# First stage of a filter-and-spectrum kernel on one core: tails and row transform in one PSUM pair ahead of the second column block, normalisation mid-step, input loaded and measured four images at a time

## The reference, cut to what matters

```
x = x + L0(gn(x), f)          # layer 0: the first stage of the kernel
x = x + L1(gn(x), a1 .. d2)   # layer 1: spectrum of gn(x), small complex products, inverse spectrum

gn(v):   mean and variance over groups of 4 channels (32 groups), (v - m) / sqrt(s + 1e-5)
L0(v,f): upsample by 2 with a 12-tap filter, columns then rows -> 266 x 266
         y = y if y >= 0 else 0.01 * y
         filter and keep every second sample, columns then rows -> 128 x 128
```

## Time and profile before

| | us |
|---|---|
| time, median of 3 runs | 5614.12 (5610.11 to 5619.64) |
| the profiled execution's own time | 5615.34 |
| its span, first to last instruction | 5613.4 |
| PE / DVE / ACT / POOL busy in the span | 4717.3 / 3792.0 / 3255.8 / 2574.6 |
| first stage: first and last step's `Z` instruction (L615, 256 of them) start at | 46.2 and 3137.5 |
| TensorE's clock granted over the span | 0.966 of full speed |

### The profile page before, as it was taken

How to read it: one execution, slowest core, us unless ns; L and a number is a source line. 1 busy time by engine, 2 the same in 40 slices (tenths; PEclk the granted TensorE clock), 3 DMA queues, 4 the chain that set the end, 5 groups by cost and what they waited for, 6 DMA issues and landing times. The chain is left out here.

```text
span 5613.4 us, 246109 instructions
## 1 busy us (share of the span) xinstructions
PE 4717.3 (84%) x103206; PEld 4285.6 (76%) x103206; DVE 3792.0 (68%) x5737; ACT 3255.8 (58%) x5654; POOL 2574.6 (46%) x2950
## 2 busy tenths in 40 slices
PE   6788787887787787888888769999999999998999
PEld 5777777777777777777777658888888888888999
DVE  5666666666666666666666588888888888884333
ACT  5655655656556656556565356666666666663332
POOL 5665656656656656656566133333333333331000
PEclk9999999999999999999999789999999999999999
DMA  1113132131131131131311412222222222225999
GB/s 52 48 48 96 48 89 62 48 96 48 57 97 48 48 104 48 55 89 48 103 49 46 140 46 75 75 75 75 75 71 69 69 75 75 75 75 227 420 421 399
DMA packets 606871, 555.75 MB, mean 99 GB/s; under 512 B 14916, under 2 KB 540228, under 8 KB 589508
## 3 DMA queue, kind: packets, MB, share of 16 engines
q1 hardware_dynamic: 606276, 546.68, 29.5%
HBM read 278.19 MB, written 268.44 MB: 97 GB/s over the span
## 5 line engine op out<-in xcount | busy, mean ns | idle before, releaser
L1278 DVE TENSOR_TENSOR Ml<-ring,Mh 128x1024 f16<-128x1024 f32 x1024 | 1199.5, 1219 | 200.5 <-ACT Mh L1245 192.9
L1245 ACT ACTIVATE Mh<-ring 128x1024 f16<-128x1024 f32 x1024 | 987.0, 1023 | 301.1 <-PE ring L1179 300.5
L753 DVE SCALAR_TENSOR_TENSOR Y<-ring,Y 128x532 f16<-128x532 f32 x1024 | 680.4, 706 | 680.1 <-ACT Y L604 680.1
L604 ACT ACTIVATE Y<-ring 128x532 f16<-128x532 f32 x1024 | 573.1, 612 | 897.6 <-PE ring L361 897.6
L345 PE MATMUL ring<-uth,g 64*128 64x138 f16 x6144 | 458.1, 227 | 545.7 <-DVE Zt L776 379.6
L1179 PE MATMUL ring<-wcur,b_hi 64*128 64x128 f16 x16384 | 747.9, 217 | 177.8 <-DVE Ml L1278 138.5
L262 POOL TENSOR_TENSOR A<-Af,A 128x788 f16<-128x788 f32 x512 | 861.9, 1683 | 41.3
L345 PEld LDWEIGHTS ring<-uth,g 64*128 64x128 f16 x6144 | 331.3, 97 | 624.8 <-DVE Yt L772 419.0
L1179 PEld LDWEIGHTS ring<-wcur,b_hi 64*128 64x128 f16 x16384 | 609.7, 94 | 248.1 <-DVE Ml L1278 156.2
L1179 PE MATMUL ring<-wcur,b_lo 64*128 64x128 f16 x8192 | 715.5, 216 | 0.0
L361 PE MATMUL ring<-uth,A 64*128 64x138 f16 x12288 | 581.7, 225 | 29.0 <-issue 25.5
(11 more groups left out here) (153 smaller groups left out, 10927.3 us busy)
## 6 DMA issues: line engine op xcount, KB each, us to landing
xb<-in_x SPq DMA_DIRECT2D x128, 512.0 KB, 4.1
x<-x1b SPq DMA_DIRECT2D x64, 1024.0 KB, 7.0
spec<-sp_out SPq DMA_DIRECT2D x256, 256.0 KB, 3.4
xin<-spec SPq DMA_DIRECT2D x128, 512.0 KB, 6.6
fd<-ft SPq DMA_DIRECT2D x128, 512.0 KB, 4.4
F<-fd SPq DMA_DIRECT2D x64, 1024.0 KB, 20.1
xq<-x SPq DMA_DIRECT2D x64, 1024.0 KB, 16.9
out<-yq SPq DMA_DIRECT2D x64, 1024.0 KB, 18.5
```

What stands on the lines that cost most here:

```text
L604: act.activation(Y[:, e, 0, m], ring[:, pr[u], :, 0:UPS], ACT.Relu).then_inc(e_yh, 1)
L753: dve.scalar_tensor_tensor(out=Y[:, e, 1, m], in0=ring[:, pr[u], :, 0:UPS], scalar=0.0, in1=Y[:, e, 0, m], op0=ALU.max, op1=ALU.subtract). ...
L1245: act.activation(hi, ps, ACT.Copy).then_inc(e_hi, 1)
L1278: dve.tensor_tensor(lo, ps, hi, ALU.subtract).then_inc(e_lo, 1)
```

## The change

Five things are changed in `phase1`, all of them together:

- **Units.** The order of the nine units becomes `U0, U1, R0, DN, TF, U2, U3, R1, DC`. TF holds the tails of both kinds in its first bank and the row transform of `x1b` (L499) in its second, and the row transform is done right behind the tails, ahead of U2. DC holds the filter back along the columns alone; R1 stands ahead of it and so takes over DN's pair, R0 takes R1's of the step before, DN takes DC's.
- **Order on PE.** The second pass of U0 comes ahead of R0, the second pass of U2 ahead of R1. `x_sums` moves to the end of the step before (k mod 4 = 1 instead of 2).
- **Normalisation mid-step.** ACT does `ground` right behind the first `a_copy`, ahead of Z, and `G` ahead of the second two Y.
- **Statistics.** DVE measures one quad of `x` in each step (behind the low halves of the tails) instead of two in each of two steps out of four; the mask of `Yc` moves behind the second two low halves of Y; `stats_copy` moves to the end of step k mod 4 = 1, `stats_out` stands behind the measure of `x1b` in step k mod 4 = 2, and POOL's `variance` ahead of its second `split_a` in step k mod 4 = 1.
- **Loads.** SP loads one quad per DMA (256 KB), as soon as the quad in its place has been used; there is a semaphore for each of the eight places, and two more loads at the end.

```diff
-        U0, U1, R0, DN, TL, U2, U3, FC, R1 = range(9)
+        U0, U1, R0, DN, TF, U2, U3, R1, DC = range(9)
...
             def body(t, jq, s6):
-                for i in range(4):
-                    sp.wait_ge(e_x1, 8 * t + 2 + 2 * i)
-                    load(4 * t + 4 + i, i)
-                    if i % 2 == 1:
-                        store(2 * t + i // 2, i // 2)
+                for i in range(SLOTS):
+                    sp.wait_ge(e_x1, 8 * t + 1 + i)
+                    load(8 * t + 8 + i, i)
+                    if i % HALF == HALF - 1:
+                        store(2 * t + i // HALF, i // HALF)
...
 # POOL
             def step(q, k, nxt=True, half=None, ground=True):
-                if half is not None and k % HALF == 2:
-                    variance(half)
                 if nxt:
                     split_a(q + 1, k + 1, 0)
                 if ground:
                     split_g(q + 2, k + 2)
                 if nxt:
                     split_tail(q + 1, k + 1)
+                if half is not None and k % HALF == 1:
+                    variance(half)
+                if nxt:
                     split_a(q + 1, k + 1, 1)
...
 # PE
                     up_cols(q, k, 1, pr[U1], 0)
+                    up_cols(q, k, 0, pr[U0], 1)
                 if nxt:
                     pe.wait_ge(e_gl, q + 2)
-                    wait(pe, e_x1, q - 1)
-                    wait(pe, e_g, q - 2)
+                    pe.wait_ge(e_af, 2 * q + 2)
                     free(3)
                     up_rows(q + 1, k + 1, 0, pr[R0], 0)
                 if up:
-                    up_cols(q, k, 0, pr[U0], 1)
                     up_cols(q, k, 1, pr[U1], 1)
...
                 if down:
-                    if up:
-                        pe.wait_ge(e_af, 2 * q + 2)
...
+                    wait(pe, e_x1, q - 1)
+                    if summed is not None:
+                        pe.wait_ge(k_tot, summed + 1)
                     free(4)
                     down_rows(q, o, pr[DN])
-                if next_half is not None:
-                    pe.wait_ge(e_af, 2 * q + 3)
-                    x_sums(next_half, pr[U3])
...
-                    tails(e, o, pr[TL], up, down)
+                    tails(e, o, pr[TF], up, down)
+                if rows:
+                    pe.wait_ge(e_x1, q - 1)
+                    for m in range(IMGS):
+                        mm = pe.matmul(ring[:, pr[TF], 1, 128 * m:128 * m + 128], x1b[:, (k - 2) % SLOTS, m, :],
+                                       dfth[:], start=True, stop=True)
+                    mm.then_inc(p_s5, 1)
...
                     up_cols(q, k, 3, pr[U3], 0)
+                    up_cols(q, k, 2, pr[U2], 1)
                 if nxt:
-                    pe.wait_ge(e_ytl, q + 1)
                     if down:
-                        pe.wait_ge(e_ztl, q)
+                        pe.wait_ge(e_zl, q)
                     up_rows(q + 1, k + 1, 1, pr[R1], 0)
                 if up:
-                    up_cols(q, k, 2, pr[U2], 1)
                     up_cols(q, k, 3, pr[U3], 1)
                 if nxt:
                     up_rows(q + 1, k + 1, 1, pr[R1], 1)
+                if up:
+                    pe.wait_ge(e_ytl, q + 1)
                 if down:
+                    pe.wait_ge(e_ztl, q)
+                    wait(pe, e_g, q - 1)
+                    linear_cols(k - 1, pr[DC])
                     pe.wait_ge(e_zl, q)
-                if rows:
-                    pe.wait_ge(e_x1, q - 1)
...
+                    down_cols(o, pr[DC])
+                if next_half is not None:
+                    x_sums(next_half, pr[DC])
...
 # ACT
                     a_copy(q + 1, k + 1, 0, pr[R0])
+                if next_half is not None and k % HALF == 2:
+                    root(next_half)
+                if half is not None:
+                    ground(q + 2, k + 2, half)
                 if down:
                     act.wait_ge(p_s3, q)
...
+                if rows:
+                    act.wait_ge(p_s5, q - 1)
+                    act.activation(G[:, :, bass.ds(4 * j5, IMGS)],
...
                 if up:
                     y_high(2, U2)
                     y_high(3, U3)
-                if half is not None:
-                    ground(q + 2, k + 2, half)
+                if next_half is not None and k % HALF == 1:
+                    squares(next_half)
                 if nxt:
                     a_copy(q + 1, k + 1, 1, pr[R1])
...
 # DVE
                 if half is not None and k % HALF == 2:
-                    stats_copy(half, pr[U3])
+                    stats_out(half, (k // HALF + 1) % 2)
...
+                if stats is not None:
+                    x_stats(*stats)
+                if up:
+                    y_low(2, U2)
+                    y_low(3, U3)
+                if batch is not None:
+                    batch_in(batch)
                 if up:
                     dve.wait_ge(e_ytl, q + 1)
                     wide = [TR, 2, IMGS, TAIL]
                     dve.tensor_tensor(Yc[:, e], Yt[:, e, :, 256:UPS].unsqueeze(2).to_broadcast(wide),
...
-                if half is not None and k % HALF == 2:
-                    stats_out(half, (k // HALF + 1) % 2)
-                if up:
-                    y_low(2, U2)
-                    y_low(3, U3)
-                if batch is not None:
-                    batch_in(batch)
-                if half is not None and k % HALF < 2:
-                    x_stats(half, loads, (k // HALF + 1) % 2, k % HALF)
                 if down:
...
+                if half is not None and k % HALF == 1:
+                    stats_copy(half, pr[DC])
```

More of the change, by code:

```diff
@@ L144, in phase1 @@
         c_up = sem("c_up")
-        x_ld = [sem(f"x_ld{n}") for n in range(4)]
+        x_ld = [sem(f"x_ld{n}") for n in range(SLOTS)]
         x1_st = [sem("x1_st0"), sem("x1_st1")]
@@ L242, in drain, with last @@
                     sp.wait_ge(sp_st[e], 32 + 2 * 16 * B * UNITS6 // 4)
-            steps(sp, first, body, lambda: store(62, 0), drain)
+            def last():
+                for i in range(2):
+                    sp.wait_ge(e_x1, NQ - SLOTS + 1 + i)
+                    load(NQ - SLOTS + i, i)
+                store(62, 0)
+            steps(sp, first, body, last, drain)
         @block.gpsimd
@@ L417, in down_cols, with step @@
                               lambda v: dth[:, v, LO * t:LO * t + hi - lo])
-            def down_cols_tail(o, pr):
-                bank = ring[:, pr, 0, :]
                 pairs(bank.rearrange("p (i w) -> p i w", i=IMGS)[:, :, TL0:W], lambda v: Zt[:, o, v, :],
                       lambda v: dtailh[:, v, 0:IMGS * TLN], stop=True).then_inc(p_s4, 1)
-            def step(q, k, up=True, nxt=True, down=True, rows=True, next_half=None, after=None):
+            def step(q, k, up=True, nxt=True, down=True, rows=True, next_half=None, summed=None, after=None):
                 e, o = k % 2, 1 - k % 2
@@ L493, in step, with spectra @@
                     up_rows(q + 1, k + 1, 1, pr[R1], 1)
+                if up:
+                    pe.wait_ge(e_ytl, q + 1)
                 if down:
+                    pe.wait_ge(e_ztl, q)
+                    wait(pe, e_g, q - 1)
+                    linear_cols(k - 1, pr[DC])
                     pe.wait_ge(e_zl, q)
[L496 to L508 removed]
+                    down_cols(o, pr[DC])
+                if next_half is not None:
+                    x_sums(next_half, pr[DC])
+            def spectra(b, q, half):
                 pe.wait_ge(e_g, QUADS * (b + 1))
@@ L516, in spectra @@
                     elif j == 1:
+                        if q is not None:
+                            pe.wait_ge(e_af, 2 * q + 4)
                         pe.wait_ge(b_x, b + 1)
@@ L548, in first @@
                 for q in range(4):
-                    step(q, q, down=q >= 1, rows=q >= 2, next_half=1 if q == 2 else None)
+                    step(q, q, down=q >= 1, rows=q >= 2, next_half=1 if q == 1 else None,
+                         summed=1 if q == 2 else None)
             def body(t, jq, s6):
                 for k in range(8):
-                    q = 8 * t + 4 + k
-                    step(q, k + 4, next_half=2 * t + 2 + k // HALF if k % HALF == 2 else None,
+                    q, half = 8 * t + 4 + k, 2 * t + 2 + k // HALF
+                    step(q, k + 4, next_half=half if k % HALF == 1 else None, summed=half if k % HALF == 2 else None,
                          after=s6 if k == 6 else None)
                     if k == 5 and s6 is not None:
-                        spectra(s6, q)
+                        spectra(s6, q, half)
             def last():
@@ L660, in first @@
                 for q in range(4):
-                    step(q, q, down=q >= 1, rows=q >= 2, j5=q - 2, next_half=1 if q == 2 else None,
-                         half=(q + 2) // HALF)
+                    step(q, q, down=q >= 1, rows=q >= 2, j5=q - 2, next_half=1, half=(q + 2) // HALF)
             def body(t, jq, s6):
```

(14 more changed lines are left out.)

83 lines of the change are left out of this document (27 added, 56 removed).

## The result

The changed kernel takes 5246.23 us (median of 4 runs, 5237.66 to 5247.99) against 5612.11 for the kernel before, run beside it: a ratio of 0.9347, 95% interval 0.9327 to 0.9366. The range of the prediction, 5030 to 5255, holds it by 9 us; the narrower range of its main forecast, 5080 to 5190, does not, and the predicted 5135 is 111 us too low.

The account below looks back on a forecast made before the run. No engine was full; PE was nearest, busy 8.39 of a 10.55 us step, with two stalls. Steps fall from 11.31 to 9.42: 1.89 x 255 = 482 off 5615 gives 5133, say 5135; range 5030 to 5255.

Parts of the forecast that it names:

- main forecast: The whole kernel takes 5135 us, own range 5080 to 5190, chance 0.55.
- Z becomes the wait: Rival, chance 0.14: if ACT comes 0.5 late or passes wait 0.2, every step pays 0.5 at R1; 5262 us.
- R0: Unit R0 in each step: its wait for the split of g and for x1b, 0.76 us, goes entirely.
- R1: Unit R1 in quiet steps: its 1.81 stall goes; Z needs 2.50 from DN's end, PE 2.51; 0.05 stall kept.
- The quiet step: A step without statistics on PE: 7.98 + 0.30 + 0.06 + 0.05 = 8.39 us, where it was 10.55.
- self waits: Second passes wait for PE's own first pass, four times a step: 0.075 each, 0.30 a step.
- height change: Going between full-height and half-height blocks, with the row transform ahead of U2: between 0 and 0.12, taken as 0.06.
- Statistics: One step in four: nmr waits for POOL's subtraction and R1 stalls 2.3; x_sums takes 0.55 of PE, same price.
- nmr finds the gap: Rival, chance 0.20: nmr gets between POOL's cast and subtraction, the statistics step's stall is some 1.15; 5025 us.
- Clock: PE's slow clock over the first stage: 0.20 a step, bounds 0 and 0.43.
- Loop return: PE's 0.95 stand for instructions every 8 steps, until now mostly under R0's wait, is bare: 0.12 a step.
- Loads and mask: 256 KB loads arrive in time, cost 0 (slower rival 0.04); Yc's mask stays short (rival 5440 us, 0.04).

Follow-up runs that it names:

- experiment 3: Changed kernel with ground moved back behind the third Y eviction on ScalarE, ahead of the first copy of A: 5272.98 us, 0.9397.
- experiment 5: Changed kernel with the row transform back behind R1's second pass and G back behind ScalarE's second copy of A: 5871.18 us, 1.0459.
- experiment 4: Changed kernel with U0's second pass moved back behind R0's first pass: 5231.77 us, 0.9319.
- experiment 2: Changed kernel with nmr made by four one-column multiplies with a scalar instead of one multiply of two SBUF tiles: 5168.15 us, 0.9213.
- experiment 6: Changed kernel with ground behind Yt, ahead of G, only in the one step of four where a block's statistics end: 5109.12 us, 0.9101.
- experiment 11: Kernel of experiment 7 with all steps of TensorE's first stage written out, so it never jumps back there: 4976.60 us, 0.8863.
- Experiment 1: Changed kernel with TensorE's inner loop over three bodies of a batch written out, the last loop too: 5155.19 us, 0.9179.
- experiment 12: Changed kernel with 128 semaphore increments, run once, put in on TensorE to move its loop code; its time is not given in the text.
- experiment 7: Changed kernel with four edits together, those of Experiment 1, experiment 2, experiment 4 and experiment 6: 4989.53 us, 0.8883.
- experiment 8: Changed kernel with the edits of Experiment 1, experiment 2 and experiment 6, U0's passes left side by side: 4998.65 us, 0.8899.
- experiment 10: Changed kernel with no branch hint on TensorE's inner loop inside the batches; the other loops keep theirs: 5263.54 us, 0.9375.

## Why the prediction held, and where it was off

The mechanism of the stage was right: both waits of the quiet step went. That the range holds the time owes something to luck: its upper end, 5255, was set by the rival "Z becomes the wait" (5262), which did not come, and the misses below took that room.

**R0, right.** The wait is gone from the quiet step; experiment 3 brings a wait for g of 0.88 back in most steps by ground's place alone. What the new PSUM pair gives was not tried by itself.

**R1, right, and as narrow as told.** No wait in quiet steps: R1 starts 2.62 behind DN's end, where the chain to Z was to take 2.50. Experiment 5 shows that the balance stands on the 0.99 of the row transform.

**The quiet step, 0.13 too short**: 8.39 forecast, 8.52 measured. The self waits were to cost 0.30 in four places; between the same starts as in the earlier trace rows the passes of U0 to U3 take 1.85 now where 1.44 was counted, 0.41 more, and experiment 4, which undoes two of the four places, gives 0.18 back where they had been set at 0.15. The height change took 0.10 (0.06 forecast), the stall of 0.05 is none. So the step adds up: 10.55 before, less the two waits of 2.57, plus 0.41, 0.10 and 0.03 in small differences, is 8.52. "Z becomes the wait" did not come.

**Statistics, right in mechanism.** nmr ends 0.01 behind POOL's subtraction; R1 waits 1.81, where 2.3 was forecast. "nmr finds the gap" did not come; experiments 2 and 6 take the cost away in other ways, by a nmr that does not wait for POOL and by a Z that does not wait for nmr. The whole cycle of four steps is 36.70 against 36.41, 0.07 a step.

**Clock, right in size.** 9.79 a step, less 36.70 / 4 and less the 0.41 of the returns (below), leaves 0.21 for it; forecast 0.20. It is a remainder, with all small errors in it. Of the 181 us of half clock 119 lie behind R1's wait in steps with statistics, as forecast, and the other 61 in the steps with PE's returns or right behind them, of which the forecast says nothing. Its "waits of at most 1.6 us each" is the wait of the earlier trace rows; PE's list of the kernel before has waits on issue of up to 3.2 as well, although 51 of its 74 stretches at half clock begin in neither a step with a return nor the one behind it.

**Loop return: the term that failed.** "Now it is bare: 0.12 a step" took the 0.95 of the earlier trace rows over. Every eighth step, in which PE's loops return or end, averages 11.83 against 8.52, 3.31 in eight steps: 0.41 a step, 0.29 more than forecast, 72 us over 248 steps. Some 0.04 of the 0.41 are not the returns': without any return, in experiment 11, these steps are still 0.35 longer than the quiet ones. The term was wrong twice: the row was one gap of one return, where a second of 0.51 followed (the waits on issue were 1.33 in such a step on average before, partly under R0's wait: the step was 1.16 longer than that four steps later); and the size belonged to the old place of the code, which the change moves (2.03 on average now, with the waits put down to POOL 2.6). Experiment 1 takes 91 us out this way, experiment 12 moves the cost elsewhere.

**Steps with spectra, counted like the others**: they were to gain 1.89 each and lost 0.61, 17 us over seven. With ground off Z's path they take 41.0 and 41.2 on average (experiments 3 and 6): the stats step that lies in the same stretch ate most of the gain. But with the edits together (experiments 7, 8 and 11) they take 42.5, 42.5 and 42.0 again, most with 2.3 to 3.4 us at half clock and with waits for the spectra's output of up to 2.9; why is open.

**The sum of the misses**: returns 72, quiet steps with statistics 0.07 x 248 = 17 and clock 2, spectra 17, and the mean of before, 11.31 of one batch where the stage has 11.27, 9 to 10: some 118, less the 4 of the earlier start, 114, where 111 is missing.

**Loads and mask, nearly as forecast**: 256 KB land in 2.9 us (page of the changed kernel), and DVE waits for a load seven times in the stage, each time in the first or second step behind spectra, 4.3 us in all. Yc takes 0.22 (0.41 to 0.92 in six of 256 steps). How near the loads are to being late was not tried; the loads and the spread of the measures over the steps were not undone by themselves.

## What to carry to other kernels

Moving a normalisation ahead so that the next consumer finds it ready paid here only in the steps where its own inputs were ready; in the others it should stand behind whatever the bound engine waits for next: placed by step, ground gave 137 us. A loop's return on an engine that is full costs what its place in the code makes of it (a step 0.3 to 5.9 us longer here), so read all the returns, not one, after each edit, not from the kernel before, and write the loop out where it is bare. And a term that balances to the hundredth deserves its own experiment: the same matmuls 2.5 us later cost 625 us, in part because the gaps also cost clock.

## What the runs showed of the hardware

- A step with a hinted return is 0.3 to 5.9 us longer, with the place of the code (changed kernel and experiment 12), and 5.5 longer without a hint where it was 3.8 with it (experiment 10); at the inner loop's end, where the hinted branch is not taken, it is 2.6 longer with the hint than without.
- The instruction packets of 16 KB go with the returns: 512 in the changed kernel, 464 with no return left, 494 where the inner returns in the batches cost 0.4 (experiment 12).
- One product of two SBUF tiles waits for POOL's running subtraction (1.20 for four columns); four products with a scalar column run during it (0.58).
- Behind 35 of 63 waits of TensorE for Z, of 1.60 to 1.84 us each, the granted clock stood at 1.2 GHz (119 of the stage's 181 us), behind the others at 2.4; behind the waits of 1.2 in experiment 2 it stood at 2.4 each time but in two steps with spectra. With two gaps in each step (experiment 5) 648 us of the stage were at 1.2 GHz, with all edits and no return left (experiment 11) 21.
